# Operands of a Strassen product formed by GpSimd inside the attention stage instead of the first expert's stage, with the early output chunks added two tiles apart

## What is computed

```
x = x + tanh(g_xattn) * (softmax(q k^T / 4) v Wo + bo)     16 heads of 16, q from layernorm(x), k and v from ctx
logits = layernorm(x) @ gate_weight.T                      4096 tokens x 8 experts
kth    = sort(logits.ravel())[4*256*6 - 1]
gates  = logits * (logits >= kth)
h      = gelu(layernorm(x) @ w1[e].T + b1[e])              hidden 1024, for every expert e
out    = x + tanh(g_ffn) * sum_e gates[:, e] * (h @ w2[e].T + b2[e])
```

## Time and profile before

| | us |
|---|---|
| median of 3 runs | 2035.85 (2035.27 to 2036.93) |
| the profiled execution's own time | 2033.89 |
| its span | 2032.1 |
| TensorE busy | 1911.8 (94%) |
| VectorE busy | 1338.6 (66%) |
| GpSimd busy | 161.3 (8%) |

### The profile page before, as it was taken

One profiled execution on the slowest core, in us unless ns is written; L12 is line 12 of the kernel. 1 busy time (PEld: TensorE's weight loads), 2 busy tenths in 40 slices (PEclk: granted clock), 3 DMA queues, 4 the chain that ended last, 5 costly groups with the idle time before them and its releaser, 6 DMA issues.

```text
span 2032.1 us, 30886 instructions
## 1 busy us (share of the span) xinstructions
PE 1911.8 (94%) x8916; PEld 1365.3 (67%) x8916; DVE 1338.6 (66%) x2333; ACT 1240.3 (61%) x2076; POOL 161.3 (8%) x334
## 2 busy tenths in 40 slices
PE   7989998999957989999999999999999999999998
PEld 5743333333336767788788878878877887887886
DVE  6588888888718886556655656565566556656555
ACT  4447776767722232576766667676666666667664
POOL 4301011101115530000000000000000000000000
PEclk9979999999968999999999999999999999999999
DMA  6833322222101324224222332322423224332221
GB/s 239 329 116 82 82 79 75 72 71 76 49 23 43 145 99 183 104 107 158 103 90 104 116 130 104 109 104 84 169 96 109 104 84 144 121 109 84 104 104 52
DMA packets 97309, 221.31 MB, mean 109 GB/s; under 512 B 31330, under 2 KB 49508, under 8 KB 87908
## 3 DMA queue, kind: packets, MB, share of 16 engines
q1 hardware_dynamic: 97124, 219.12, 31.3%
HBM read 178.57 MB, written 40.24 MB: 108 GB/s over the span
## 4 chain that ended last, share of the span: by engine, by line
PE 61%; DVE 4%; issue 2%; POOL 2%; ACT 1%; DVEq 0%; ACTq 0%
PE ps_y L2117 29%; PE ps_h L2064 26%; PE ps_y L2036 3%; PE ps_h L2022 3%; DVE h_hi L2388 1%; DVE h_lo L2392 1%; ACT gelu L2280 1%; DVE out_T_acc L2469 1%; DVE early L2526 0%; DVE w_pair L2518 0%; DVE gated L2462 0%; DVE t_lo L2439 0%; POOL t_sum L1958 0%; POOL t_sum L1962 0%; POOL t_sum L1954 0%
## 5 line engine op out<-in xcount | busy, mean ns | idle before, releaser
L2392 DVE TENSOR_TENSOR h_lo<-gelu,h_hi 128x512 fp32r<-128x512 f32 x512 | 359.9, 707 | 406.4 <-ACT h_hi L2283 403.6
L2064 PE MATMUL ps_h<-x_hi,w_pair 128*128 128x512 f32 x1568 | 570.0, 397 | 14.8 <-ACT gelu L2280 7.1
L2280 ACT ACTIVATE gelu<-early,b 128x512 f32<-128x512 f32 x336 | 243.2, 724 | 238.6 <-DVE early L2526 235.3
L2117 PE MATMUL ps_y<-h_hi,w_hi 128*128 128x512 f32 x896 | 355.1, 396 | 3.5 <-DVE h_lo L2392 3.5
L2064 PEld LDWEIGHTS ps_h<-x_hi,w_pair 128*128 128x128 f32 x1568 | 295.9, 189 | 91.6 <-ACT gelu L2280 9.9
L2117 PE MATMUL ps_y<-h_hi,w_lo 128*128 128x512 f32 x896 | 354.9, 396 | 0.0
L2117 PE MATMUL ps_y<-h_lo,w_hi 128*128 128x512 f32 x896 | 354.1, 395 | 0.0
L963 DVE TENSOR_REDUCE low<-ps_s 128x1 f32<-128x512 f32 x512 | 321.6, 682 | 35.7 <-PE ps_s L820 34.1
L2064 PE MATMUL ps_h<-x_lo,w_pair 128*128 128x512 f32 x784 | 310.2, 396 | 0.0
L2283 ACT ACTIVATE h_hi<-gelu 128x512 fp32r<-128x512 f32 x448 | 283.4, 633 | 18.1
L2526 DVE TENSOR_TENSOR early<-ps_h,copy 128x512 f32<-128x512 f32 x336 | 230.2, 685 | 64.0 <-PE ps_h L2064 63.0
(11 more groups left out here) (247 smaller groups left out, 2169.8 us busy)
## 6 DMA issues: line engine op xcount, KB each, us to landing
x_hi<-blocks_scratch SPq DMA_DIRECT2D x28, 1024.0 KB, 5.1
x_lo<-blocks_scratch SPq DMA_DIRECT2D x28, 1024.0 KB, 8.8
x_hi<-blocks_scratch SPq DMA_DIRECT2D x28, 768.0 KB, 6.8
x_lo<-blocks_scratch SPq DMA_DIRECT2D x28, 768.0 KB, 10.3
gate<-gates_scratch SPq DMA_DIRECT2D x64, 256.0 KB, 3.2
q_st<-q_scratch SPq DMA_DIRECT2D x192, 64.0 KB, 2.2
k_st<-k_scratch SPq DMA_DIRECT2D x192, 64.0 KB, 2.3
k_scratch<-k_hl SPq DMA_DIRECT2D x8, 1024.0 KB, 3.9
```

Source lines behind the costliest of these rows:

```text
L2064: mm = pe.matmul(bank, w[wp], x[xp], start=start and n == 0, stop=n == 2, skip_group_check=not start)
L2117: mm = pe.matmul(ps_y[s][:, d, :], w[:, j, at], h[:, c, :], start=(i == 0 and c < 2 and m == 0), stop=(i == QUADS - 1 and c >= 2 and m == 2))
L2280: act.activation(gelu[:, c % GELUS, :], src, ACT.Gelu_apprx_tanh, bias=b1[p][:, j:j + 1]).then_inc(gelu_done, 1)
L2392: dve.tensor_tensor(h_lo[:, j % RING, :], gelu[:, j % GELUS, :], h_hi[:, j % RING, :].bitcast(F32), ALU.subtract).then_inc(h_ready, 1)
```

## The change

The sums of twins 0, 1 and 2 are formed during attention, by GpSimd alone, and stored from there. Twin 3 is left to expert 0, where GpSimd does each of its 18 operations behind one tile. ScalarE and VectorE no longer split blocks. The low part overwrites t_sum. GpSimd's attention loop is written out, with the bias of batch b + 1 added ahead of the sums. The gates are turned one tile later (GATES_AT), and the early chunks are added behind tiles 38, 39, 42, 44 and 46 (ADD_AT, counted from 32) instead of 37, 38, 39, 40 and 42. A branch that is not taken here forms the sums in build_experts if attention was clipped.

```diff
+def first_sums(pool, keep, t_sum, twin, step, base, hold=lambda i: None):
+    b11, b12, b21, b22, t1, t2, t3, t4 = block_parts(keep, t_sum, twin)
+    done = base + twin * BLOCK_STEPS
+    hold(0)
+    pool.tensor_tensor(t1, b12[0], b11[0], ALU.subtract).then_inc(step, 1)
+    hold(1)
+    pool.tensor_tensor(t3, b22[0], b12[0], ALU.subtract).then_inc(step, 1)
...
+def split_blocks(pool, t_hi, t_sum, zero, twin, step, base, hold=lambda i: None):
+    done = base + twin * BLOCK_STEPS + 10
+    pool.wait_ge(step, done)
+    for i in range(CELLS):
+        hold(10 + i)
+        pool.tensor_tensor(t_hi[:, i, :], t_sum[:, i, :], zero[:].to_broadcast([P, SEQ]), ALU.add).then_inc(step, 1)
+    for i in range(CELLS):
+        pool.wait_ge(step, done + i + 1)
+        hold(14 + i)
+        pool.tensor_tensor(t_sum[:, i, :].bitcast(F32R), t_sum[:, i, :], t_hi[:, i, :].bitcast(F32), ALU.subtract).then_inc(step, 1)
...
@@ build_attend, SyncE
                     if exists(ahead[0]) and exists(b):
                         load_group(*ahead)
+                    if twin is not None and g == 3:
+                        store_blocks(sp, scratch, keep, t_hi, t_sum, twin, t_step, t_stored)
                     ahead = group_after(b, g, 1)
                     if exists(ahead[0]) and exists(b):
                         send_lows(*ahead)
...
+            with sp.Fori(1, TWINS - 1) as bb:
+                batch(bb * 2)
+                batch(bb * 2 + 1, bb - 1)
+            batch(BATCH - 2)
+            batch(BATCH - 1, TWINS - 2)
...
@@ build_attend, GpSimd
-            with pool.Fori(0, BATCH) as b:
-
+            add_bias(0)
+            for b in range(BATCH):
                 reciprocal_root(b)
+                if b % 2 == 0 and b >= 2:
+                    pool.wait_ge(lows_checked, group_no(b + 1, 2) + 2)
+                    split_blocks(pool, t_hi, t_sum, zero, b // 2 - 1, t_step, 0)
+                if b + 1 < BATCH:
+                    add_bias(b + 1)
+                if b % 2 and b + 1 < BATCH:
+                    pool.wait_ge(taken["xnT"], (b + 1) * KT)
+                    wait(pool, t_stored, b // 2 * BLOCK_STORES)
+                    pool.wait_ge(lows_checked, group_no(b + 1, 3) + 2)
+                    first_sums(pool, keep, t_sum, b // 2, t_step, 0)
+                    pool.wait_ge(lows_checked, min(group_no(b + 2, 0) + 2, BATCH * GROUPS))
+                    last_sums(pool, keep, t_sum, b // 2, t_step, 0)
...
+GATES_AT = 1
+ADD_AT = (6, 7, 10, 12, 14)
-SPLIT_AT = (8, 18, 28, 38)
...
@@ build_experts, GpSimd
+            def after_tile(i):
+
+                pool.wait_ge(h_ready, RING + SUM_TILES + i)
+
+            first_sums(pool, keep, t_sum, TWINS - 1, t_step, 0, after_tile)
+            last_sums(pool, keep, t_sum, TWINS - 1, t_step, 0, after_tile)
+            split_blocks(pool, t_hi, t_sum, zero, TWINS - 1, t_step, 0, after_tile)
...
@@ build_experts, VectorE
-            chunk(0, SEARCH, None, range(LEAD, HT - SEARCH + 1))
+            for n in range(LEAD, 2 * HT):
+                c, j = SEARCH + n // HT, n % HT
+                halves(0, c, j)
+                extra(c, j)
+                if n in ADD_AT:
+                    i = ADD_AT.index(n)
+                    if first_order[i] < KEPT_CHUNKS:
+                        add_early(first_order[i], i)
+                    else:
+                        gate_chunk(0, 0, first_order[i], first_order[i] % 2, i, tile_no(0, first_order[i], HT) + RING)
+                        if i > 1:
+                            add_gated(0, first_order[i])
+                if n == ADD_AT[1] + 1:
+                    add_gated(0, first_order[1])
```

More of the change, by code:

```diff
@@ L53 @@
 STORES = 16 * 3
+BLOCKS = 7
+CELLS = 4
+TWINS = BATCH // 2
+SUM_TILES = 6
+B11, B21, B22, T1, T2, T3, T4 = range(BLOCKS)
+STAGED = (T1, T2, T4, T3)
+BLOCK_STEPS = 10 + 2 * CELLS
+BLOCK_STORES = 8 * 16
 def wait(eng, sem, value):
@@ new lines, in store_blocks @@
+def store_blocks(sp, scratch, keep, t_hi, t_sum, twin, done, stored, base=0):
+    sp.wait_ge(done, base + twin * BLOCK_STEPS + BLOCK_STEPS)
+    for part, staged in enumerate((t_hi, t_sum)):
+        x = keep[("x_hi", "x_lo")[part]]
+        to = scratch["blocks"][bass.ds(twin, 1), part]
+        first = twin * 2 * SEQ
+        staged = flat(staged).bitcast(F32) if part == 0 else flat(staged)
+        for k, at, size, src in ((0, 0, 1, x[:, 0, bass.ds(first, SEQ)].bitcast(F32)),
+                                 (1, 0, 2, x[:, 1, bass.ds(first, 2 * SEQ)].bitcast(F32)),
+                                 (0, 1, 3, staged[:, 0:3 * SEQ]), (1, 2, 1, staged[:, 3 * SEQ:])):
+            sp.dma_start(to[:, :, k, at * SEQ:(at + size) * SEQ].rearrange("a p t -> (a p) t"), src).then_inc(stored, 16)
@@ L1868, in _ @@
                 sp.wait_ge(turned, BATCH)
+                for twin in range(TWINS - 1):
+                    store_blocks(sp, scratch, keep, t_hi, t_sum, twin, stats_done, std_done, BATCH * TT)
+                sp.wait_ge(std_done, BATCH + (TWINS - 1) * BLOCK_STORES)
             w2_rows = io["w2T"][0].rearrange("(j p) d -> p j d", p=P)
@@ L1875, in _ @@
             load_w2(1)
-            for twin in range(TWINS - 1):
-                store_blocks(twin)
             sp.wait_ge(gates_T_ready, 1)
@@ L1931, in _ @@
             pool.wait_ge(consts_set, 7)
+            clip = pool.value_load(keep["clip_flag"][0:1, 0:1], min_val=0, max_val=1)
+            with pool.If(clip > 0):
+                pool.wait_ge(lo_done, BATCH)
+                for twin in range(TWINS - 1):
+                    wait(pool, std_done, BATCH + twin * BLOCK_STORES)
+                    first_sums(pool, keep, t_sum, twin, stats_done, BATCH * TT)
+                    last_sums(pool, keep, t_sum, twin, stats_done, BATCH * TT)
+                    split_blocks(pool, t_hi, t_sum, zero, twin, stats_done, BATCH * TT)
+                pool.wait_ge(std_done, BATCH + (TWINS - 1) * BLOCK_STORES)
             def split(half, skip):
```

145 lines of the change are left out of this document (54 added, 91 removed).

## The result

| | before | after |
|---|---|---|
| median of 20 runs | 2034.76 us (2031.32 to 2040.07) | 2040.57 us (2029.95 to 2049.08) |
| ratio, 95% interval | | 1.0031 (1.0018 to 1.0043) |
| profiled execution's own time | 2033.89 | 2043.78 |
| its span | 2032.1 | 2042.0 |
| mean granted clock over the span | 0.972 | 0.959 |

The account below looks back on a forecast made before the run. TensorE, busy 94%, was taken as the bound, so savings count only where it waits. Gains of 18.7 us less losses of 12.3 gave net 6.4: 2029.5 us for the median against 2035.85, range 2020 to 2037.

Parts of the forecast that it names:

- the one on the clock: Attention: a low-clock stretch costs 2.8 us and may follow a new stall; none was counted in the sum.
- My rival for this: Five new attention stalls (three splits, two stores) each bring a low-clock stretch of 2.8 us: 2043.5, slower; chance 0.13.
- my own signs of being wrong: Search above 2.95 us a round, or attention growing by less than 5 or more than 20 us.
- Splits: Attention, group 2 of batches 3, 5, 7: GpSimd's splits hold layer_norm's pairs and TensorE waits; loss 8.1 us.
- Stores: End of batches 3 and 5: eight stores delay send_lows, so TensorE waits at batches 4 and 6; loss 3.7 us.
- Sums: Attention, group 0 of batches 3, 5, 7: ten sums make three pairs of comparisons late; loss 0.5 us.
- nobody waits for a comparison: Attention: late comparisons cost little because only GpSimd and SyncE wait for them; part of the 0.5 us loss.
- First expert: Gains from search, gates and added chunks, less the new branch: 18.7 us.
- Gates and additions: First expert: gates turned one tile later gain 2.2 us; added chunks spread over nine tiles gain 4.7 us.
- the floor that I had taken: First expert's search: 2.90 us a round, from eight rounds in which GpSimd forms nothing; search gain 12.8 us.
- the step on the branch: First expert: GpSimd's jump over a block ahead of the weights' splits delays the first h_lo; loss 1.0 us.

Follow-up runs that it names:

- e4: The change without sums, splits or block stores in attention; SyncE stores plain parts for twins 0 to 2 in the first expert: 2015.27 us, 0.9898 of before.
- e6: e4 with one useless VectorE addition ahead of the second pair of layer_norm in every batch, a planted stall: 2030.09 us, 0.9976 of before.
- e5: The change with splits behind group 3's comparisons and stores behind send_lows in group 1 of the next batch: 2012.05 us, 0.9895 of before.
- e13: e5 with the first six sums behind the comparisons of group 0, the last four behind those of group 1: 2012.52 us, 0.9881 of before.
- e1: The change with the stores behind send_lows and the splits directly behind the ten sums: 2028.03 us, 0.9971 of before.
- e2: The change with the stores alone moved behind send_lows, splits still beside layer_norm: 2030.73 us, 0.9993 of before.
- e14: e5 run again unchanged, on the same chip as e13: 2013.68 us, 0.9895 of before.
- e8: The kernel before with the change's GATES_AT and ADD_AT alone, sums and splits still in the first expert: 2030.08 us, 0.9973 of before.

## Why the prediction was wrong

**The step that failed** is the one on the clock: "It may follow a new stall; in my sum none does." I had priced the low clock at nothing. Of attention's growth of 28.8 us in the profiled pair, 17.4 is longer busy time for the same matmuls: 6.1 in the three groups 2, 3.6 in the first groups of batches 4 and 6, 1.0 in groups 0, and 6.7 in the last group, whose cause is open. In length, the clock added 3.2 to the groups 2 and 3.1 to the first group of batch 6. Not all of the 17.4 comes from stalls: e4, which added none, was busy 6.3 more than the kernel before, by its stretches at the starts of batches and in the last group.

In the change the low stretch stood behind eight of nine split stalls and in the first group of batch 6 in three profiles of three; e6 makes such stretches with stalls alone, five times of seven; e5 and e13, with all the work kept and these stalls gone, have none in groups 1 and 2, and the first group of batch 6 at 1.00. Of 20 runs of the change, those with a lower mean clock are the longer ones (correlation -0.88), from 2029.95 to 2049.08. That holds within the kernel before as well (-0.91 to -0.98), so by itself it gives no cause; but the change's mean clock is 0.962 where the kernel before has 0.968 to 0.970, which at 1.1 to 1.35 us for 0.001, the slopes of these sets of runs, is an estimated 7 to 10 us.

My rival for this had the mechanism and nearly the time (2043.5). The time was partly luck: it had five stretches at 2.8, 14.0 in all, where the clock behind the five stalls added 6.7 (0.8, 2.0, 0.5, 0.4 and 3.1), the last group added 5.6 that it did not name, the stores' waits were 3.8 too small in it, and the first expert gained 4.3 more. I gave it 0.13 because a wait of 2.03 in the first expert is followed by a clock of 1.00. That was a poor witness: TensorE is busy without a break around that wait, while in attention it waits many times a group (busy 11.68 of 13.31). That this difference decides is argued, not tested.

Two of my own signs of being wrong came: attention grew by more than 20, and the search's 31 rounds average 3.05, above 2.95, by its first two rounds.

**Splits**: 9.4 against 8.1, right in size by luck, since two errors met. What VectorE's held pairs cost TensorE was 2.3, 2.3 and 1.5, 6.2 in all, where I had 3.4, 3.4 and 1.3. The order of the delays was as I said: in batch 3 the first pair ended 1.0 late, the second, behind it, 2.3 late; but each was held less than the 1.4 and the further 2.0 of my term. The other 3.2 was clock, which I had left out. The Trainium skill (page "SBUF — State Buffer", section "Who interferes with whom") held for layer_norm's tensor_scalar, 0.73 a pair and then 1.73 and 2.07, and also for the comparisons with two inputs in SBUF.

**Stores**: 10.9 against 3.7, where 7.5 is waiting. What was mis-sized is the delay. At batch 6 the eight issues took 7.4 instead of 6.7 and send_lows' own two 2.41 instead of 1.32; at batch 4, before and then after:

```profile
336.20 1.36 SPq L721 DMA_DIRECT2D q_st<-low_rows  x2
```

```profile
344.28 2.55 SPq L805 DMA_DIRECT2D q_st<-low_rows  x2
```

So send_lows ended 9.3 later at batch 4, and by about 9 later at both batches when set against TensorE's own progress, where I had 6.7. That is most of the way from my 1.0 to 3.5 at batch 4 and from my 2.7 to 3.8 at batch 6, where the product followed the issue by 1.6 us, sooner than I had. The 2.18 that TensorE waited at batch 4 before was not a wait for the rows: they had been issued by 337.56, 7.7 us ahead of the product, while after the stores the product follows 2.2 behind the issue. It stands there (1.84 to 2.36) in all nine profiles with no stores around it, in eight of them with "issue" as its releaser, where TensorE's loop over three batches starts anew; the profile doesn't say what it waits for. In e1 and e2, with the stores behind send_lows, it is 3.19 and 3.94.

**Sums**: 2.7 against 0.5 in the account; 1.2 to 2.0 a batch by e13 and e14, 4.8 in all, part of which the account hides: batch 3 had a low stretch in that group before and none after. The error was "nobody waits for a comparison".

**First expert**: 23.0 against 18.7. Gates and additions came as priced, though e8 shows that the gates needed the sums to be gone. The search's rounds came down to the floor that I had taken, from the third sum on. Tiles 0 to 31 gained 15.9 where I had 11.8, and the step on the branch seems to have had the sign wrong. VectorE's first split of w_first took 2.12 and 2.74 beside GpSimd's before; after, GpSimd starts 1.05 later behind its branch, and VectorE's take 0.42 and 0.69. The first eight tiles are 5.9 shorter; how much of that is the branch and how much the sums of twin 0 was not separated.

**Open** is why the last group of attention was 2.7 to 5.6 longer than before in the change's three profiles (-0.1 in e5 and e14, 2.3 in e13). In the profiled pair all of it is busy time (36.68 against 29.97, at a clock of 0.56 against 0.69). A low stretch from the split stall in batch 7 reaches into it, but e2 has that stall too and only 1.5, and e4 and e13, without the stall, are 1.2 and 2.3 longer, so part of it is chance.

## What to carry to other kernels

In a stage like this attention, where TensorE is busy with many short waits, price a new stall at one to two and a half times its length: its own time, and the lower clock that may follow (2.3 became 3.1 to 4.4 here, 1.1 became 1.1 to 2.7). Splits that made no stall were free even at 9 us in a group. Before placing GpSimd work, list VectorE's instructions with two SBUF inputs and its casts and tensor_scalars out of SBUF, however small, and ask what is queued behind each. And when transfers are put ahead of a small one, price the small one's own issue anew: it took 2.4 to 2.6 here instead of 1.3.
